# Experts in units of 128 rows instead of tiles of 256, a feed-forward that alternates its two layers by chunk, and a regrouped start and tail

## The chip, the cores and the metric

The kernel runs on one core of one Trainium2 chip. The time is the device time of one execution in microseconds (us); a row of a profile tells times from the first to the last instruction of the profiled execution (its span). The engines are TensorE (PE, with PEld for its weight loads and PEldq for its sequencer, the queue that feeds it), VectorE (DVE), ScalarE (ACT), GpSimd (POOL) and SyncE (SP, which only issues DMAs).

## The reference, cut to what matters

Two blocks are added to x (16 x 256 rows of 256 numbers, with a small vector for each of 16 sequences): a block of a recurrence and a sparse feed-forward, then a block of a mixture and a quantised feed-forward.

```python
# x: (16, 256, 256) f32, cond: (16, 256) f32
# block 1
h_new = tanh(h * (1 - alpha) + sigmoid(h @ Wh.T + z_t @ Wz.T + b) * z_t)     # 256 steps in turn
hs    = all h                                                                # 4096 rows
idx   = top_2(softmax(hs @ gate_w + gate_b))                                 # of 8 experts
h1    = relu(hs @ w1[e] + b1[e])                                             # 256 -> 1024
x     = x + sum over the row's two experts of (h1 @ w2[e] + b2[e])           # 1024 -> 256
# block 2
m     = (shared gated network + two of eight small experts, by sigmoid gates) / 3
q(v)  = clip(round(v / s), 0, 255) * s,  s = max(max(v), 1e-8) / 255         # one s for a whole tensor
h     = relu(q(m) @ wq1.T + bq1)                                             # wq: int8 by row
out   = x + q(h) @ wq2.T + bq2
```

## The kernel before, in words

The program has five stages: the recurrence (to 381 us), the experts (to 814), the mixture (from 829 to 1137), the first pass of the quantised feed-forward (to 1191), which finds the largest hidden value, and its second pass (to 1254), which computes the output. The stages share one program for each engine; each engine runs its instructions in the order in which they stand, and waits for numbered semaphores.

**Experts.** During the recurrence the rows of each expert are scattered into regions of `ROOMS` places in memory. The stage then handles 39 tiles (`SLOT_TILES`) of `ST` = 256 places, so that no tile holds rows of two experts. Which expert a tile has is known only at run time: `value_load` (L1097) brings its number into a register, and the addresses of weights are worked out from it by TensorE's sequencer. `slot_tiles` (L1059) writes out 15 tiles (`JOBS`), loops over 11 x 2 (`Fori`) and writes out the last 2. In each tile:
- TensorE, `experts_pe` (L1079): first layer (L1105), 8 chunks `f` of 128 hidden numbers, each 6 matmuls with `W1` stationary and the tile's 256 rows moving (fp16 high and low parts of weights and rows, without low by low); then 8 transposes of the next tile's rows (L1086); then the second layer (L1117), 8 x 3 x 2 matmuls with `hid` stationary, `SQ` = 2 blocks of 128 rows, and 256 columns of `W2` moving. `hid` and `W1` and their kin are parts of the buffers `lane` and `W`.
- ScalarE: the copy of the transposed rows `xT` (L1129), and for each chunk the relu from `ps` to one of 4 buffers `v4` (L1141). It signals `l1_v`.
- VectorE, `experts_dve` (L1190): for each chunk the high part (L1208) and the low part (L1210) of `hid`, signalling `l1_hid`; the results of the tile before (L1198, signalling `out_ready`, for which the second layer waits); in tiles written out, jobs (`split_piece`, `scale_piece`, `quantise_piece`) that prepare weights of later stages.
- SyncE loads rows (L1406) and biases; GpSimd stores the results by a scatter for each block of 128 rows (L1284) and, in early tiles, scatters rows and pads.

**Feed-forward.** Groups of 512 rows, 8 in all. First pass: ScalarE scales a group (L940) and copies its transposed rows (L935); TensorE transposes (L871) and computes two groups per `row_max` (L875, matmuls L883); VectorE takes maxima (L986). Second pass: `group` (L915) runs all 8 chunks of `hidden` (L906, matmuls L911) of the next group, then waits for the output bank (`ob_s`) and runs all 32 output matmuls (L924) of its own. ScalarE scales and rounds (L955, L952), VectorE casts (L1022) and writes outputs (L1010, L1014). At the end GpSimd adds each group to the result in memory by an accumulating DMA (L1055); `x` was stored there before by SyncE (L1459).

**Start.** SyncE loads all of the recurrence's weights, `h0`, `alpha` and the bias before `z`; TensorE starts when all of VectorE's preparations (`prep`) are done. The first loads of the experts' weights (`stage`, issued behind them on SyncE's queue) are needed by ScalarE (L1506) in the first step.

## Time and profile before

| | us |
|---|---|
| median of 3 runs | 1268.68 (1264.85 to 1269.13) |
| profiled execution, its own time | 1267.8 |
| its span, first to last instruction | 1264.8 |
| experts' stretch (381 to 814) | 433 |
| mean granted clock of TensorE | 0.987 |

The profile is of one execution whose own time lies within 0.1% of the median; 3.0 us of it lie around the span. "busy" is the time in which an engine's instructions ran, also while they overlapped; the chain of waits follows the work that ended last backwards through what released it. A row of the sequencer (PEldq) counts register operations, which aren't in the busy time of any engine. Instructions named ISA in an order of instructions are register operations of an address, FUSED_REGOPS in the trace.

### The profile page before, as it was taken

Reading aid. Unit: us, or ns where it says so; the run is one execution under the profiler, and the core shown is the slowest. Engines: PE = TensorE matmul, PEld = TensorE weight load, DVE = VectorE, ACT = ScalarE, POOL = GpSimd, SP = SyncE. Lnnn points to the kernel's source line nnn. Section 1 sums busy time; section 2 is a strip of 40 time slices with the busy share of each in tenths; the row PEclk is TensorE's granted clock in tenths of the full one; section 3 lists DMA queues with packets and bytes.
Section 4 is the critical chain, followed back from the end, with each engine's and each line's share of the span. In section 5 each row is a group of like instructions: output and inputs, shape, how many; then the busy total and the mean of one; then the engine's idle time right before and its main releaser. Section 6 shows DMA issues by size and latency. Waiting matters only on the chain.

```text
span 1264.8 us, 32645 instructions
## 1 busy us (share of the span) xinstructions
PE 1123.6 (89%) x10732; PEld 864.7 (68%) x10733; DVE 892.9 (71%) x3002; ACT 583.3 (46%) x1782; POOL 250.9 (20%) x289
## 2 busy tenths in 40 slices
PE   6777777787768999999999999889999999987895
PEld 4665666565557999998899999746766666763263
DVE  5677677676775587965555555468898889987875
ACT  3555555555553444444444444362445533434373
POOL 1002112112114675343333333300000000001001
PEclk9999999999999999999999999989999999998998
DMA  6222333233233475343333333243000000000035
GB/s 174 76 72 89 90 97 97 82 93 109 71 91 106 102 166 133 91 70 59 58 53 60 62 62 62 36 132 134 2 1 1 0 1 0 1 1 1 1 51 83
DMA packets 57527, 84.36 MB, mean 67 GB/s; under 512 B 7361, under 2 KB 47170, under 8 KB 57410
## 3 DMA queue, kind: packets, MB, share of 16 engines
q1 hardware_dynamic: 41186, 57.94, 16.1%
q0 software_dynamic: 16224, 24.96, 10.9%
q8 instruction: 62, 1.02, 0.3%
q14 instruction: 55, 0.45, 0.1%
HBM read 51.36 MB, written 35.70 MB: 69 GB/s over the span
## 4 chain that ended last, share of the span: by engine, by line
PE 75%; ACT 9%; DVE 9%; issue 3%; DMA 1%; SPq 1%; POOL 0%; DVEq 0%; ACTq 0%; POOLq 0%
PE ps L570 23%; PE ps L1105 16%; PE ps L1117 16%; PE ps L1660 7%; DVE ps L1589 5%; PE ps L1665 4%; ACT work L1516 4%; ACT ps L1511 3%; DVE imax L986 2%; PE ps L924 2%; PE ps L1630 1%; PE ps L1086 1%; ACT W L955 1%; PE ps L1638 1%; PE ps L911 1%
## 5 line engine op out<-in xcount | busy, mean ns | idle before, releaser
L1141 ACT ACTIVATE lane<-ps,b_now 128x256 f32<-128x256 f32 x312 | 147.4, 474 | 240.1 <-PE ps L1105 216.4
L1105 PE MATMUL ps<-lane,W 128*128 128x256 f16 x1872 | 213.3, 274 | 2.2 <-ACT lane L1129 1.3
L1117 PE MATMUL ps<-W,lane 128*128 x1872 | 210.7, 273 | 0.0
L1105 PEld LDWEIGHTS ps<-lane,W 128*128 x1872 | 184.0, 98 | 25.1 <-issue 2.8
L1117 PEld LDWEIGHTS ps<-W,lane 128*128 128x128 f16 x1872 | 181.5, 98 | 20.4
L1660 PE MATMUL ps<-work 128*128 128x16 f16 x2048 | 99.1, 177 | 89.5 <-ACT work L1516 88.8
L1660 PEld LDWEIGHTS ps<-work 128*128 128x128 f16 x2048 | 76.3, 107 | 141.3 <-ACT work L1516 139.9
L1284 POOL DMA_INDIRECT results<-lane,dest x78 | 123.8, 1588 | 231.3 <-DVE lane L1198 195.8
L570 PE MATMUL ps<-W,work 128*128 128x512 f16 x768 | 168.7, 382 | 0.0
L1210 DVE TENSOR_TENSOR lane<-lane 128x256 f16<-128x256 f32 x312 | 133.4, 427 | 10.8
L570 PEld LDWEIGHTS ps<-W,work 128*128 128x128 f16 x768 | 74.9, 98 | 90.1 <-issue 2.2
L570 PE MATMUL ps<-work,W 128*128 128x256 f16 x1152 | 127.1, 273 | 0.0
L570 PEld LDWEIGHTS ps<-work,W 128*128 128x128 f16 x1152 | 112.4, 98 | 13.1
L1198 DVE SCALAR_TENSOR_TENSOR lane<-ps,b_now 128x512 f32<-128x512 f32 x39 | 26.9, 690 | 127.7 <-PE ps L1117 127.7
L1208 DVE CAST lane<-lane 128x256 f16<-128x256 f32 x312 | 90.5, 290 | 24.4 <-ACT lane L1141 24.3
L1630 PE MATMUL ps<-work 128*128 128x128 f32 x256 | 98.3, 490 | 7.5 <-DVE gw_s L1565 7.5
L1603 DVE TENSOR_TENSOR work<-ps,work 128x32 f16<-128x32 f32 x256 | 48.9, 191 | 78.1 <-ACT ps L1518 77.8
L834 DVE SCALAR_TENSOR_TENSOR W<-ps,comb,W 128x256 f32 (+1 forms) x256 | 101.5, 475 | 1.9 <-PE ps L570 1.9
L1589 DVE TENSOR_TENSOR_SCAN ps<-ps,work 128x64 f32<-128x64 f32 x256 | 76.4, 298 | 34.3 <-ACT ps L1511 11.5
L1254 POOL DMA_INDIRECT rows<-work,slot_of x64 | 62.9, 982 | 156.3 <-DVE ps L1589 152.3
L1576 DVE SCALAR_TENSOR_TENSOR work<-ps,alpha,work 128x16 f32<-128x16 f32 x510 | 93.3, 224 | 0.0
L1511 ACT ACTIVATE ps<-ps 128x32 f32<-128x32 f32 x256 | 46.6, 182 | 97.9 <-PE ps L1665 96.7
(214 smaller groups left out, 1533.7 us busy)
## 6 DMA issues: line engine op xcount, KB each, us to landing
lane<-rows SPq DMA_DIRECT2D x39, 257.0 KB
stage<-in_w1T SPq DMA_DIRECT2D x16, 512.0 KB, 3.7
stage<-in_w2T SPq DMA_DIRECT2D x16, 512.0 KB, 4.0
b_now<-in_b SPq DMA_DIRECT2D x39, 128.0 KB
work<-in_zT SPq DMA_DIRECT2D x32, 128.0 KB, 2.2
results<-in_xn SPq DMA_DIRECT2D x32, 128.0 KB
W<-results SPq DMA_DIRECT2D x8, 512.0 KB, 3.8
out<-W SPq DMA_DIRECT2D x8, 512.0 KB, 4.9
```

Source lines behind the costliest of these rows:

```text
L570: last = pe.matmul(dst, lhs(a, k), rhs(b, k), start=(n == 0 and k == ks[0]), stop=(n == 2 and k == ks[-1]))
L834: dve.scalar_tensor_tensor(y[:, GT * g + q], ps[:, bank_of(U_PAIR + GT * p + q), j * D:(j + 1) * D], comb[:, q, 2 * p + j:2 * p + j + 1], ...
L1105: last = pe.matmul(ps[:, f % 4, 0:ST], of_e(W1[:, bass.ds(e, 1), a, k, f * P:(f + 1) * P]), xT[:, p, b, k], start=(i == 0 and k == 0), sto ...
L1117: last = pe.matmul(ps[:, 4 + q, 0:D], hid[:, a, f, q * P:(q + 1) * P], of_e(W2[:, bass.ds(e, 1), b, f]), start=(i == 0 and f == 0), stop=( ...
L1141: act.activation(v4[:, f % 4], ps[:, f % 4, 0:ST], ACT.Relu, bias=b1_now[:, p, f:f + 1], scale=A_SCALE / W_SCALE).then_inc(l1_v, 1)
L1208: dve.tensor_copy(hid[:, 0, f], v4[:, f % 4]).then_inc(split0, 1)
L1210: dve.tensor_tensor(hid[:, 1, f], v4[:, f % 4], hid[:, 0, f], ALU.subtract).then_inc(l1_hid, 1)
L1284: pool.indirect_dma_start(out=results_d, in_=obuf[:, p, q], in_offset=None, compute_op=ALU.add, out_offset=bass.IndirectOffsetOnAxis(ap=de ...
L1576: dve.scalar_tensor_tensor(zs[:, j % 2, c // BATCH, k, :, 1], h[:, k], alpha[:, k:k + 1], z[:, j, k, c:c + BATCH], ALU.mult, ALU.add).then ...
L1589: dve.tensor_tensor_scan(ps[:, 5, 0:2 * DB], ps[:, 6, 0:2 * DB], zs[:, j % 2, s % STEPS_PER_TILE].rearrange("p c b v -> p (c b v)"), 0.0, ...
L1630: pe.matmul(dst, wz[:, k, cols], z[:, slot, k, :], start=(k == 0), stop=False, skip_group_check=True)
L1660: pe.matmul(ps[:, b + m, c:c + BATCH], w[:, k, m * P:(m + 1) * P], hring[:, prev, 0, k, pc:pc + BATCH], start=False, stop=False, skip_grou ...
```

## The change

- Experts: `ST` 128, so `SLOT_TILES` 71, `JOBS` 29 (31 units written out, 40 in the loop), `EARLY` 32. The second layer's accumulator has two banks by turns, so TensorE waits for the results of the unit before last. ScalarE writes 8 buffers `v8`; VectorE makes high and low parts of two chunks (`PAIR`) at once. Jobs, rows and pads are spread one a unit; each unit has one scatter of results.
- Second pass: for each chunk TensorE runs `hidden(g + 1, f)` and then the 4 outputs of chunk `f` of its own group; the last group runs its two halves one behind the other. The wait for `ob_s` stands ahead of both.
- First pass: `row_max(0)` begins with the first group's half; the transposes of later groups stand between its chunks; ScalarE's order is scale 0, scale 1, copy 0, copy 1, scale 2, and so on.
- Tail: the last two groups (`ADDED` = 6 are still accumulated) are made complete by VectorE (x with bias added ahead, `x_with_bias`, behind group 1's hidden chunks) and stored by SyncE. The mixture's last maximum is taken by halves.
- Start: `z`'s first part and the preparation of `Wz` come ahead of all but the weights' load; TensorE begins with `z`'s products.

```diff
-ST = 256
+ST = 128
 SLOT_TILES = (PAIRS + E * (ST - 1)) // ST
-JOBS = 15
-EARLY = 16
+JOBS = 29
+EARLY = 32
+PAIR = 2
@@ experts_pe, second layer
-                if not is_tile(n, 0):
-                    pe.wait_ge(out_ready, n)
+                if not (is_tile(n, 0) or is_tile(n, 1)):
+                    pe.wait_ge(out_ready, n - 1)
                 for f in range(FC):
-                    pe.wait_ge(l1_hid, FC * n + f + 1)
+                    if f % PAIR == 0:
+                        pe.wait_ge(l1_hid, FC // PAIR * n + f // PAIR + 1)
                     for i, (a, b) in enumerate(((0, 0), (1, 0), (0, 1))):
                         for q in range(SQ):
-                            last = pe.matmul(ps[:, 4 + q, 0:D], hid[:, a, f, q * P:(q + 1) * P],
+                            last = pe.matmul(ps[:, 4 + SQ * p + q, 0:D], hid[:, a, f, q * P:(q + 1) * P],
@@ experts_act
-                    act.activation(v4[:, f % 4], ps[:, f % 4, 0:ST], ACT.Relu, bias=b1_now[:, p, f:f + 1],
+                    act.activation(v8[:, f], ps[:, f % 4, 0:ST], ACT.Relu, bias=b1_now[:, p, f:f + 1],
@@ experts_dve
-                    dve.tensor_copy(hid[:, 0, f], v4[:, f % 4]).then_inc(split0, 1)
-                    dve.tensor_tensor(hid[:, 1, f], v4[:, f % 4], hid[:, 0, f], ALU.subtract).then_inc(l1_hid, 1)
+                    dve.tensor_copy(hid[:, 0, pair], v8[:, pair]).then_inc(split0, 1)
+                    dve.tensor_tensor(hid[:, 1, pair], v8[:, pair], hid[:, 0, pair], ALU.subtract).then_inc(l1_hid, 1)
@@ ffn_pe, first pass
-                pe.wait_ge(yq_T, 2 * n + 2)
+                pe.wait_ge(yq_T, 2 * n + 1)
...
+                        if f == 0 and m == 1:
+                            pe.wait_ge(yq_T, 2 * n + 2)
...
+                    if f in (2, 5) and 2 * n + 2 + f // 5 < GROUPS:
+                        transposes(2 * n + 2 + f // 5)
@@ ffn_pe, second pass
             def group(g, buf):
-                if not is_last(g):
-                    hidden(g + 1)
                 if not is_tile(g, 0) and not is_tile(g, 1):
                     pe.wait_ge(ob_s, 2 * (g - 1))
...
+                else:
                     for f in range(FC):
+                        hidden(g + 1, f)
+                        wait_rounded(pe, g, f)
+                        for q in range(GT):
+                            last = output(buf, f, q)
@@ ffn_dve
+            def x_with_bias(g):
+                xg_ = x1[:, GT * g:GT * g + GT]
+                dve.tensor_tensor(xg_, xg_, bq2.rearrange("p (a d) -> p a d", a=1).broadcast_to([P, GT, D]), ALU.add)\
+                   .then_inc(xb_ready, 1)
@@ SyncE, end
+            for n in range(2 * ADDED, 2 * GROUPS):
+                sp.wait_ge(ob, n + 1)
+                sp.dma_start(out[:, 2 * n:2 * n + 2], y[:, 2 * n:2 * n + 2]).then_inc(last_out, 16)
@@ SyncE, start
             sp.dma_start(wst, WT).then_inc(w_in, 16)
-            sp.dma_start(h0[:], h0T).then_inc(w_in, 16)
-            sp.dma_start(alpha[:], alphaT).then_inc(w_in, 16)
+            sp.dma_start(z[:, 0], zT[:, 0]).then_inc(z_in[0], 16)
@@ TensorE, start
-            pe.wait_ge(prep, 8)
+            pe.wait_ge(prep, 2)
```

The first place is TensorE at the head of a tile, the load of the expert's number and the first layer's first chunk. Before (W and lane are the stationary and the moving operand's buffers, the last numbers the instruction's shape):

```order
L1097 TENSOR_LOAD expert_of
L1097 ISA x2
L1105 ISA [waits l1_v,xT_ready]
L1105 MATMUL ps<-lane,W 128x256
L1105 ISA
L1105 MATMUL ps<-lane,W 128x256 x3
L1105 ISA
L1105 MATMUL ps<-lane,W 128x256
L1105 ISA
L1105 MATMUL ps<-lane,W 128x256
```

After:

```order
L1141 TENSOR_LOAD expert_of
L1141 ISA x2
L1149 ISA [waits l1_v,xT_ready]
L1149 MATMUL ps<-lane,W 128x128
L1149 ISA
L1149 MATMUL ps<-lane,W 128x128 x3
L1149 ISA
L1149 MATMUL ps<-lane,W 128x128
L1149 ISA
L1149 MATMUL ps<-lane,W 128x128
```

The same operations stand there in the same number; each matmul moves half as many columns.

The second place is TensorE between the two layers, the transposes and the second layer's first chunks. Before:

```order
L1086 MATMUL ps<-identh,lane 128x128 [waits xg_in0]
L1086 MATMUL ps<-identh,lane 128x128 x7
L1117 ISA [waits l1_hid,out_ready]
L1117 MATMUL ps<-W,lane 128x256 x4
L1117 ISA
L1117 MATMUL ps<-W,lane 128x256 x2
L1117 ISA [waits l1_hid]
L1117 MATMUL ps<-W,lane 128x256 x4
```

After:

```order
L1130 MATMUL ps<-identh,lane 128x128 [waits xg_in1]
L1130 MATMUL ps<-identh,lane 128x128 x3
L1162 ISA [waits l1_hid,out_ready]
L1162 MATMUL ps<-W,lane 128x256 x2
L1162 ISA
L1162 MATMUL ps<-W,lane 128x256
L1162 ISA
L1162 MATMUL ps<-W,lane 128x256 x2
L1162 ISA
L1162 MATMUL ps<-W,lane 128x256
```

The transposes are 4 for 8, and between two register operations stand half as many matmuls; the wait for `l1_hid` comes once for two chunks.

The third place is TensorE in the second pass, in the first group: the hidden layer of group 1 (L911 before, L926 after) and the output of group 0 (L924, L931). Before:

```order
L911 MATMUL ps<-W,lane 128x512 [waits hb_h]
L911 MATMUL ps<-W,lane 128x512
L911 MATMUL ps<-W,lane 128x512 [waits hb_h]
L911 MATMUL ps<-W,lane 128x512
L924 MATMUL ps<-lane 128x256 [waits hb_qd] x8
L924 MATMUL ps<-lane 128x256 x24
L911 MATMUL ps<-W,lane 128x512 [waits hb_h]
L911 MATMUL ps<-W,lane 128x512
```

After:

```order
L926 MATMUL ps<-W,lane 128x512 [waits hb_h]
L926 MATMUL ps<-W,lane 128x512
L931 MATMUL ps<-lane 128x256 [waits hb_qd]
L931 MATMUL ps<-lane 128x256 x3
L926 MATMUL ps<-W,lane 128x512 [waits hb_h]
L926 MATMUL ps<-W,lane 128x512
L931 MATMUL ps<-lane 128x256 [waits hb_qd]
L931 MATMUL ps<-lane 128x256 x3
```

Eight hidden chunks and then 32 outputs have become one hidden chunk, then 4 outputs, by turns.

## Rows read from the trace of the kernel before

**Rows 1.** Busy time (and instructions) of each engine, the experts' stretch:
```profile
core 0: us, PE busy (x) PEld busy (x) DVE busy (x) ACT busy (x) POOL busy (x), PEclk, DMA share, GB/s
381.00:814.00 433.00, 430.13 (x4071) 385.67 (x4071) 268.20 (x754) 186.55 (x354) 179.41 (x186) 1.00 0.39 81
```
**Rows 2.** Chain of waits, one tile (start us, us, what):
```profile
403.97 0.45 PE ps L1086 x8
404.42 5.24 PE ps L1117 x48
409.65 5.24 PE ps L1105 x48
```
**Rows 3.** Weight loads and sequencer by line: count, ns min/median/max, first and last start
```profile
L1105 PEld LDWEIGHTS ps<-lane,W x1872: 95/98/148, 384.0 to 807.9; 128*128 x188
...
L1105 PEldq FUSED_REGOPS  x1248: 46/46/51, 383.9 to 806.6; - x179
...
L1097 PEldq TENSOR_LOAD <-expert_of x39: 297/301/493, 381.4 to 800.9; - x39
```
**Rows 4.** The same view in short stretches, written-out tiles and loop:
```profile
L1117 PEldq FUSED_REGOPS  x15: 46/46/46, 403.2 to 408.1; - x15
...
L1105 PEldq FUSED_REGOPS  x24: 46/46/46, 409.1 to 412.0; - x24
...
L1105 PEldq FUSED_REGOPS  x32: 46/46/46, 682.1 to 686.5; - x32
...
L1117 PEldq FUSED_REGOPS  x16: 46/46/46, 686.9 to 691.4; - x16
...
L1105 PEldq FUSED_REGOPS  x10: 46/46/51, 692.6 to 694.0; - x10
```
**Rows 5.** Chain of waits in the mixture, matmuls of 128 columns:
```profile
851.73 0.89 PE ps L603 x16
```
**Rows 6.** Groups by shape, 376 to 814: busy us, mean ns, idle before:
```profile
L1210 DVE TENSOR_TENSOR lane<-lane 128x256 f16<-128x256 f32 x312 | 133.4, 427 | 10.8
L1208 DVE CAST lane<-lane 128x256 f16<-128x256 f32 x312 | 90.5, 290 | 24.4 <-ACT lane L1141 24.3
L1198 DVE SCALAR_TENSOR_TENSOR lane<-ps,b_now 128x512 f32<-128x512 f32 x39 | 26.9, 690 | 127.7 <-PE ps L1117 127.7
...
L1141 ACT ACTIVATE lane<-ps,b_now 128x256 f32<-128x256 f32 x312 | 147.4, 474 | 240.1 <-PE ps L1105 216.4 <-DVE lane L1210 10.7 <-issue 9.0
L1129 ACT ACTIVATE lane<-ps 128x1024 f16<-128x1024 f16 x39 | 39.9, 1022 | 0.4 <-PE ps L1086 0.4
```
**Rows 7.** Chain of waits, from the experts to the mixture:
```profile
814.50 1.55 POOL results L1284
...
816.36 3.79 DMA results<-lane,dest
```
**Rows 8.** Chain of waits, first pass of the feed-forward:
```profile
1139.83 3.23 ACT W L940 x3
...
1145.96 3.61 PE ps L883 x8
1149.59 5.95 DVE imax L986 x5
```
**Rows 9.** Chain of waits, second pass:
```profile
1200.14 3.49 PE ps L924 x32
1203.63 1.74 PE ps L911 x8
...
1207.65 3.49 PE ps L924 x32
```
**Rows 10.** End of the chain, and landing times of the output's DMAs:
```profile
1253.69 0.86 POOL out L1055
...
DMA to landing us min/median/max: 2.7/5.3/5.7
```
**Rows 11.** Chain of waits, start:
```profile
8.10 4.31 DMA stage<-in_w1T
```

More of the change, by code:

```diff
@@ L32 @@
 RING = 4
+ADDED = GROUPS - 2
 W_SCALE = 256.0
@@ L894, in ffn_pe @@
             largest(0)
-            for n, groups in enumerate((range(0, 3), range(3, 6), range(6, 8), ())):
-                for g in groups:
-                    transposes(g)
+            for g in range(2):
+                transposes(g)
+            for n in range(GROUPS // 2):
                 row_max(n)
@@ L904, in ffn_pe, with hidden @@
             pe.wait_ge(ia_mx, FC * GROUPS // 2)
-            def hidden(g):
-                for f in range(FC):
-                    if not (is_tile(g, 0) and f < 4):
-                        pe.wait_ge(hb_h, FC * g + f - 3)
-                    for k in range(DC):
-                        last = pe.matmul(ps[:, f % 4], w1qT[:, k, f * P:(f + 1) * P], yqT[:, k, bass.ds(GN * g, GN)],
-                                         start=(k == 0), stop=(k == DC - 1))
-                    last.then_inc(hb_ps, 1)
+            def hidden(g, f):
+                if not (is_tile(g, 0) and f < 4):
+                    pe.wait_ge(hb_h, FC * g + f - 3)
+                for k in range(DC):
+                    last = pe.matmul(ps[:, f % 4], w1qT[:, k, f * P:(f + 1) * P], yqT[:, k, bass.ds(GN * g, GN)],
+                                     start=(k == 0), stop=(k == DC - 1))
+                last.then_inc(hb_ps, 1)
@@ L915, in group, with output @@
+            def output(buf, f, q):
+                return pe.matmul(ps[:, 4 + 2 * buf + q // 2, (q % 2) * D:(q % 2 + 1) * D],
+                                 hq[buf][:, f, q * P:(q + 1) * P], w2qT[:, f], start=(f == 0 and q % 2 == 0),
+                                 stop=(f == FC - 1), skip_group_check=True)
             def group(g, buf):
-                if not is_last(g):
-                    hidden(g + 1)
                 if not is_tile(g, 0) and not is_tile(g, 1):
                     pe.wait_ge(ob_s, 2 * (g - 1))
-                for q in range(GT):
-                    for f in range(FC):
-                        if q == 0:
-                            wait_rounded(pe, g, f)
-                        last = pe.matmul(ps[:, 4 + 2 * buf + q // 2, (q % 2) * D:(q % 2 + 1) * D],
-                                         hq[buf][:, f, q * P:(q + 1) * P], w2qT[:, f], start=(f == 0), stop=(f == FC - 1))
-                    if q % 2:
-                        last.then_inc(ob_ps, 1)
@@ L929, in ffn_pe @@
-            hidden(0)
+                if is_last(g):
+                    for half in range(2):
+                        for f in range(FC):
+                            if half == 0:
+                                wait_rounded(pe, g, f)
+                            for q in (2 * half, 2 * half + 1):
+                                last = output(buf, f, q)
+                        last.then_inc(ob_ps, 1)
+                else:
+                    for f in range(FC):
+                        hidden(g + 1, f)
+                        wait_rounded(pe, g, f)
+                        for q in range(GT):
+                            last = output(buf, f, q)
+                            if f == FC - 1 and q % 2:
+                                last.then_inc(ob_ps, 1)
@@ L930, in ffn_pe @@
+            for f in range(FC):
+                hidden(0, f)
             ffn_groups(pe, group)
@@ new lines, in tile @@
+                    dve.tensor_copy(hid[:, 0, pair], v8[:, pair]).then_inc(split0, 1)
+                    dve.wait_ge(split0, FC // PAIR * n + h + 1)
+                    dve.tensor_tensor(hid[:, 1, pair], v8[:, pair], hid[:, 0, pair], ALU.subtract).then_inc(l1_hid, 1)
+                    if isinstance(n, int) and n < len(LAST_OPS):
+                        ops = LAST_OPS[n]
+                        for k in range(ops.start + 2 * h, min(ops.start + 2 * h + 2, ops.stop)):
+                            if k < ROUTE_OPS:
+                                route_op(dve, BATCHES - 1, k)
+                            else:
+                                late_table_op(dve, k - ROUTE_OPS)
@@ L1679, in step @@
                     ranks(pe, i - 1)
-            pe.wait_ge(prep, 8)
+            pe.wait_ge(prep, 2)
             pe.wait_ge(z_in[0], 16)
+            for part in range(3 * DC):
+                if part == 2:
+                    pe.wait_ge(prep, 5)
+                z_part(0, part)
             pe.wait_ge(idents, 11)
-            for part in range(3 * DC):
-                z_part(0, part)
+            pe.wait_ge(gw_split, 2)
             steps = RING * STEPS_PER_TILE
```

193 lines of the change are left out of this document (106 added, 87 removed).

## The prediction

> **What bounds the kernel now.** I read the table of stretches first. In the experts, 433 us and a third of the span, TensorE is busy 430.1 us; the next, VectorE, 62% [rows 1]. The chain of waits says the same tile for tile: 48 pairs (weight load and matmul) of the first layer 5.24 us, 8 transposes 0.45, 48 pairs of the second layer 5.24, without a gap [rows 2]. A pair with 256 columns moving is 5.24/48 = 0.109 us, a tile 10.93, and 39 tiles 426 us. By this view alone, smaller units look like a gain.
>
> The second view is TensorE's sequencer, the queue that feeds the array. The experts' weights are addressed by a register (which expert), and each change of address costs a register operation: 1248 of them in the first layer, 32 a tile [rows 3], and 16 a tile in the second [rows 4]. Where the queue runs free they come 24 in 2.9 us, 2.9/23 = 0.126 us apart, whether one matmul or three lie between them [rows 4]. In the first layer 32 take 4.0 us and the array 5.24: today the sequencer is ahead. It fills the queue and is held back by it, which costs nothing. Of this the busy shares show nothing; the question of this change is whether it stays so.
>
> **Experts, the large part.** Tiles of 256 rows become 71 units of 128. Rooms fall from 9984 to 9088. Per unit the first layer keeps 48 pairs, now with 128 columns; the second has 24 pairs with 256; 4 transposes. Array price of 128 columns with another weight each time: 16 in 0.89 us, 0.0556 each [rows 5]. A unit is 52 x 0.0556 + 24 x 0.109 = 5.51 us on the array, 71 units 391 us, 35 less than now.
>
> The register operations don't halve. The orders of instructions show the first layer's pattern unchanged (operation, 1 pair, operation, 3 pairs, operation, 1, operation, 1, for each of 8 chunks), and the second's with half the pairs behind the same 16. So the sequencer needs for a unit:
> - first layer 32 x 0.126 = 4.0 us, against 48 x 0.0556 = 2.7 for the array: the sequencer sets it;
> - from there past the transposes to the second layer's first operation 0.4 us (686.5 to 686.9) [rows 4];
> - 15 steps of 0.126, 1.9 us (array 24 x 0.109 = 2.6, but it starts with nothing in hand, behind the sequencer, and the queue hides this over the next boundary, where the sequencer is the later one);
> - from the last operation of the second layer past the load of the expert's number (0.30 us) [rows 3] to the next first layer 1.0 us (408.1 to 409.1) [rows 4].
> Sum 7.3 us for the units that are written out. In the loop the first layer's 32 take 4.4 us (682.1 to 686.5; more register arithmetic stands there), the boundary 1.2 (691.4 to 692.6) [rows 4], and I take 2.3 for the second layer with its own arithmetic: 4.4 + 0.4 + 2.3 + 1.2 = 8.3. 31 units are written out, 40 run in the loop: 31 x 7.3 + 40 x 8.3 = 558 us against 426: **+132 us**. Ends: the operation's pitch alone and a boundary half hidden, 7.0 and 8.0, give 537; waits that each add a little, 7.5 and 8.7, give 581.
>
> The other engines fit in 7.3 us. VectorE per unit: 4 x (0.29 + 0.43) [rows 6], results half of 0.69, so 3.2, and a job of at most some 3 us in some early units. ScalarE: 8 activations of 128 columns and a copy, under half of 8 x 0.47 + 1.02 [rows 6] plus fixed parts, about 4. GpSimd: one scatter of 1.55 [rows 7] where two stood, with loads of numbers; rows and pads, one a unit. The store lands 3.8 us after its issue [rows 7], with two buffers for two units. Waits that vanish (the accumulators' second bank, 8 intermediate buffers for 4) were worth nothing: TensorE never waited for them. The first unit's transposes and copy are half as long: 8 x 0.0556/2 plus half of a copy of 1.02 [rows 2, 6], -0.7, with the issue **-0.9**. The scan carries a table twice as long: 16 columns more in a few operations, **+0.4**.
>
> **Experts to mixture.** The last store is one scatter, not two: 816.36 - 814.50 = 1.86, less some of the issue behind it, with half of the results' 0.69 [rows 6, 7], **-2.1** (0 to -2.2).
>
> **First pass of the feed-forward.** Before, ScalarE scales three groups (3.23 us), then copies and scales in turn, and the first chunk starts at 1145.96 [rows 8]. Now the order is scale, scale, copy, copy: the first half may start near 1139.83 + 2/3 x 3.23 + 1.02 for a copy of 1024 columns [rows 6] = 1143.0, the second a copy later, 1144.0. From 1149.59 on VectorE's maxima set the pace (5 in 5.95 us, 1.19 each, 32 in all) [rows 8] and are what they were. So the start moves by 2 to 3 us and nothing behind it; the other transposes fall between chunks where TensorE waits for VectorE anyway. I take **-2.2**, between 0 and -3.0.
>
> **Second pass.** Now a group takes 7.51 us, from 1200.14 to 1207.65, of which the array works 3.49 in 32 output pairs and 16 x 0.218 = 3.48 in the hidden layer (8 in 1.74) [rows 9], 6.97 together. The rest is a wait for ScalarE at the seam between the two. Alternating by chunk hides it behind the output of the group before: 7 x 0.52 = 3.6 gained. Against it: the wait for the output bank (ob_s) now stands ahead of the hidden layer, and with it all of group 3's hidden chunks are queued; VectorE reaches it later by two additions of 128x1024, each 2 x 0.69 = 1.38 at most by the results' rate for 512 [rows 6]. I charge 1.6 for what of 2.7 isn't covered. The last group by halves puts up to one such addition more behind the last matmul, 0.6. At the start, group 0's output no longer waits for the last two hidden chunks of group 1, 4 x 0.218 = 0.9. Together **-2.3** (0 to -4).
>
> **Tail.** The last accumulating DMA takes 0.86 to issue and lands after 5.3 in the median; a store without accumulation lands after 2.7 at the least [rows 10]. 5.3 + 0.86 - 2.7 - 0.4 of SP's issue, **-3.0** (-1 to -4). **Start:** z's weights first lets TensorE begin earlier, but the first step waits for the load issued at 8.10 that lands 4.31 later [rows 11], and it stands as far behind in SP's queue as before: **0**. The mixture is untouched.
>
> Sum: 1267.8 + 132 - 0.9 + 0.4 - 2.1 - 2.2 - 2.3 - 3.0 = **1389.7**, by the profiled execution (span 1264.8 and 3.0 around it), which lies 0.9 under the median; 1390.
>
> **Rivals.** *A: the sequencer doesn't set the pace*, because its pitch is longer only under the profiler's recording, or the queue lets the array catch up. Then 426 - 391 = -35 and the other edits' -10.1: 1267.8 - 45.1 = **1223**. For it: today's profiled time equals the unrecorded ones, but today the sequencer has slack, so this proves nothing. Against it: 0.126 is found at each free stretch, and 48 operations a unit need 6.0 us at any order, over 5.51. It decides once the pitch falls under 5.51/48 = 0.115 with the boundaries hidden. 0.08.
>
> *B: A, but a pair with 128 columns costs more than 0.0556*, since the weight load (98 ns [rows 3], now hidden under 109) no longer fits. Upper bound 0.098: a middle of 0.077 gives 52 x 0.077 + 2.62 = 6.6 a unit, 469, +43 - 10 = **1301**. Against it: the 16 pairs of [rows 5] change weights each time too. 0.03.
> The Trainium skill, "TensorE: Matmul & The Clock Gate", section "Back-to-back issue gap", gives some 81 ns for a sustained pair of 128 columns; that would be an estimate of 6.8 us a unit and about 1315 in rival B. The trace has 0.0556 for 16 in a row, so it disagrees over short runs, and under 7.3 us a unit the rule would be hidden altogether.
>
> *C: the forecast, with a wait on top.* The second layer's last pair of chunks needs activation, cast and subtraction behind the last matmul, 0.3 + 0.29 + 0.43 and the semaphores between: 1.3 us [rows 6], and the sequencer gets there 0.4 + 1.4 behind it. If VectorE is late by results or jobs, 0.7 a unit is lost, 50 us: **1440**. 0.06.
>
> *D: the pace is as forecast but the loop's units cost what the others do*, 71 x 7.3 = 518: 1350. It lies just under the forecast's range; 0.03.
>
> **How the numbers follow.** The forecast 0.80 (1358 to 1422: the ends 537 and 581 with the small terms' ends), A 0.08, B 0.03, C 0.06, D 0.03. Faster by over 0.5% (about what a measurement of this kernel can tell) is A and a rest of others, 0.09; within 0.5% only something between A and B, 0.02; slower 0.89. The range that holds 8 in 10: 1350 to 1425.
>
> **What would show it.** In the profile after: register operations of the first layer 0.124 to 0.128 apart with the array idle between ("issue" or the sequencer as what ended the wait), a unit of 7.3 us written out and 8.3 in the loop, the experts' stretch 560 us with TensorE busy under 75% of it. The first maximum of the first pass 2 us nearer the mixture's end; groups of the second pass 7.0 us apart but for one; end of the kernel 3 us nearer the last addition. The prediction is wrong if units take 5.5 us with operations closer than 0.115 (A), if the chain names VectorE ahead of the second layer (C), or if the array's pairs are further apart than 56 ns while the sequencer is ahead (B).

## The result and the profile after

The changed kernel takes 1388.44 us (1386.84 to 1389.26) against 1267.72: the ratio is 1.0954, with an interval of 1.093 to 1.0977. It is slower by 121 us, as forecast; 1390 was predicted. The execution that was profiled took 1388.98 us and the three others 1386.84 to 1389.26, so the recording of the profile isn't what makes the kernel slow (one of the two ways in which rival A could have come true).

The spans of the two profiled executions differ by 121.7 us (1386.5 and 1264.8). Cut at the same events in both traces, that is:

| from ... to | before | after | difference | predicted |
|---|---|---|---|---|
| start to the last step of the recurrence | 380.2 | 379.5 | -0.7 | +0.4 |
| to the last matmul of the experts | 433.3 | 565.8 | +132.5 | +131.1 |
| to the mixture's first activation | 10.5 | 8.3 | -2.2 | -2.1 |
| mixture, to its last maximum | 313.7 | 315.0 | +1.4 | 0 |
| first pass | 53.7 | 50.0 | -3.7 | -2.2 |
| second pass, to the last addition | 62.1 | 60.6 | -1.5 | -2.3 |
| to the end of the span | 11.3 | 7.3 | -4.0 | -3.0 |

The busy time of the experts' stretch, which answers to [rows 1] (columns as there):

```profile
381.00:945.30 564.30, 531.28 (x5407) 416.72 (x5403) 274.68 (x727) 243.19 (x641) 172.69 (x236) 0.99 0.31 65
```

The stretch is 131 us longer, and TensorE still counts as busy for 94% of it. I had forecast under 75%, and that was wrong. A "busy" matmul of 128 columns lasts 224 ns in the records while the array takes a new one every 56 ns if it gets one. When they come 90 ns apart the records still overlap, and TensorE looks busy though it waits for its sequencer. The busy share can't tell these apart; the pitch can. The chain of waits, for two written-out units, answers to [rows 2]:

```profile
453.05 4.28 PE ps L1149 x48
457.33 0.22 PE ps L1130 x4
457.55 2.62 PE ps L1162 x24
460.17 0.06 issue
460.23 4.33 PE ps L1149 x48
```

A unit takes 460.23 - 453.05 = 7.18 us. The second layer's pairs cost 2.62/24 = 0.109 as before and the transposes 0.22/4 = 0.055. But the first layer's 48 pairs take 4.28 us, 0.089 each, where the same shape in the mixture took 0.0556 [rows 5]. The rows of the sequencer (count, ns min/median/max, first and last start), over the stage, in a first layer written out and in a first and a second layer of the loop, answer to [rows 3, 4]:

```profile
L1149 PEldq FUSED_REGOPS  x2272: 46/46/51, 382.3 to 942.1; - x190
...
L1162 PEldq FUSED_REGOPS  x1136: 46/46/46, 391.4 to 944.3; - x190
...
L1149 PEldq FUSED_REGOPS  x31: 46/46/46, 452.9 to 456.9; - x31
...
L1149 PEldq FUSED_REGOPS  x32: 46/46/51, 706.4 to 710.9; - x32
...
L1162 PEldq FUSED_REGOPS  x16: 46/46/46, 711.1 to 713.3; - x16
```

3408 operations stand where 1248 + 624 stood; 2272/71 = 32 and 1136/71 = 16 a unit. In the written-out unit 31 of them take 4.0 us (4.0/30 = 0.133 apart; the row's window ends ahead of the 32nd), in the loop 32 take 4.5. By the load of the expert's number, one unit to the next, the written-out units are 7.12 to 7.30 us apart once the first few are past (predicted 7.3), those of the loop 8.24 and 8.42 by turns, 8.33 in the mean (predicted 8.3).

### The profile page after: what moved, and what is told of

Its sections match the earlier page's. It is cut to its first block, busy times and chain, and to the rows that moved or that the text cites. A ratio compares the mean times of both kernels' runs of the same rounds, so it can differ in the third digit from the quotient of the medians.

```text
span 1386.5 us, 38626 instructions
## 1 busy us (share of the span) xinstructions
PE 1222.3 (88%) x12072; PEld 897.1 (65%) x12073; DVE 902.5 (65%) x2980; ACT 645.0 (47%) x2070; POOL 242.2 (17%) x336
## 4 chain that ended last, share of the span: by engine, by line
PE 77%; DVE 8%; ACT 7%; issue 5%; DMA 1%; SPq 0%; another core or an unknown queue 0%; DVEq 0%; ACTq 0%
PE ps L1149 23%; PE ps L576 20%; PE ps L1162 14%; PE ps L1713 7%; DVE ps L1642 4%; PE ps L1718 4%; ACT work L1566 3%; ACT ps L1561 3%; PE ps L926 2%; PE ps L931 2%; DVE imax L1017 2%; PE ps L1683 1%; PE ps L1130 1%; PE ps L897 1%; DVE W L840 1%
## 5 line engine op out<-in xcount | busy, mean ns | idle before, releaser
L1186 ACT ACTIVATE lane<-ps,b_now 128x128 f32<-128x128 f32 x568 | 207.2, 368 | 318.6 <-PE ps L1149 285.6
L1149 PE MATMUL ps<-lane,W 128*128 128x128 f16 x3408 | 325.0, 224 | 33.0 <-issue 27.5
L1149 PEld LDWEIGHTS ps<-lane,W 128*128 x3408 | 241.5, 98 | 125.7 <-issue 54.2
L1256 DVE CAST lane<-lane 128x256 f16<-128x256 f32 x284 | 86.0, 303 | 178.6 <-ACT lane L1186 168.3
L1162 PE MATMUL ps<-W,lane 128*128 x1704 | 198.8, 273 | 0.0
L1162 PEld LDWEIGHTS ps<-W,lane 128*128 128x128 f16 x1704 | 162.6, 98 | 20.9
L1325 POOL DMA_INDIRECT results<-lane,dest x71 | 112.0, 1577 | 170.8 <-DVE lane L1245 165.6
L1258 DVE TENSOR_TENSOR lane<-lane 128x256 f16<-128x256 f32 x284 | 121.1, 427 | 9.7
L1245 DVE SCALAR_TENSOR_TENSOR lane<-ps,b_now 128x256 f32<-128x256 f32 x71 | 30.1, 424 | 99.7 <-PE ps L1162 99.6
```

Source lines behind the costliest of these rows:

```text
L1149: last = pe.matmul(ps[:, f % 4, 0:ST], of_e(W1[:, bass.ds(e, 1), a, k, f * P:(f + 1) * P]), xT[:, p, b, k], start=(i == 0 and k == 0), sto ...
L1162: last = pe.matmul(ps[:, 4 + SQ * p + q, 0:D], hid[:, a, f, q * P:(q + 1) * P], of_e(W2[:, bass.ds(e, 1), b, f]), start=(i == 0 and f == 0 ...
L1186: act.activation(v8[:, f], ps[:, f % 4, 0:ST], ACT.Relu, bias=b1_now[:, p, f:f + 1], scale=A_SCALE / W_SCALE).then_inc(l1_v, 1)
L1258: dve.tensor_tensor(hid[:, 1, pair], v8[:, pair], hid[:, 0, pair], ALU.subtract).then_inc(l1_hid, 1)
L1325: pool.indirect_dma_start(out=results_d, in_=obuf[:, p, q], in_offset=None, compute_op=ALU.add, out_offset=bass.IndirectOffsetOnAxis(ap=de ...
```

## The experiments

Twelve more kernels were run. The three with addresses by constants, the two doses and the one without the loop were timed once each, the other six four to ten times; where a time is of one execution, the trace's stage stands beside it. "Stage" below is the time from the last step of the recurrence to the last matmul of the experts, from the trace; it is 433.3 before and 565.8 in the changed kernel.

### Is it the register operations?

**All of them away, units of 128.**

```diff
-                                             of_e(W1[:, bass.ds(e, 1), a, k, f * P:(f + 1) * P]), xT[:, p, b, k],
+                                             W1[:, 0, a, k, f * P:(f + 1) * P], xT[:, p, b, k],
...
-                                             of_e(W2[:, bass.ds(e, 1), b, f]), start=(i == 0 and f == 0),
+                                             W2[:, 0, b, f], start=(i == 0 and f == 0),
```

> The changed kernel, but TensorE addresses the weights of expert 0 for every unit, by constants; so all rows go through expert 0's weights, and the 48 register operations a unit are gone. The load of the expert's number and the waits stay. Sequencer theory: the array sets the pace, 52 x 0.0556 + 24 x 0.109 = 5.5 us, with the boundary (load of the number, about 1 us of the sequencer) hidden behind what is queued: units of 5.5 to 6.2 us, the stage 565 us - 71 x 1.9 = about 430, the kernel 1240 to 1290. Rival (a pair of 128 columns costs more than 0.0556 in this layer, or waits between the engines hold it): the unit stays above 6.8 us and the kernel above 1330.

Measured: 1226.99 us, against 1265.03 for the kernel before on the same chip; the stage is 406.2 us. The chain in it:

```profile
452.22 2.75 PE ps L1149 x48
454.96 0.22 PE ps L1130 x4
455.19 2.62 PE ps L1162 x24
457.81 2.75 PE ps L1149 x48
```

A unit takes 5.59 us. The first layer's pair costs 2.75/48 = 0.057 in this very layer. So the array's price of a pair was right, and the 4.28 us were not the array's. This is rival A's world (1223 predicted for it), made true by taking away what the forecast rests on.

**The same for tiles of 256**, the edit the same in the kernel before.

> The kernel before (tiles of 256), but TensorE addresses the weights of expert 0 by constants for all tiles, so all rows go through expert 0's weights; no register operations for the weights. Sequencer theory: it was ahead of the array anyway, so nothing is gained: stage 433 us, total within 4 us of before. Rival (register operations cost the array in any case): up to 48 x 0.126 = 6 us a tile less, at least -50 us in all.

Measured: 1263.21 against 1263.65, the stage 432.1 us. Taking 48 register operations from each tile gains nothing where the sequencer is ahead of the array. The two together settle it: the same edit is worth 160 us of the stage in one kernel (565.8 to 406.2) and 1.2 us in the other (433.3 to 432.1).

**Only the second layer's away, units of 128.**

```diff
-                                             of_e(W2[:, bass.ds(e, 1), b, f]), start=(i == 0 and f == 0),
+                                             W2[:, 0, b, f], start=(i == 0 and f == 0),
```

> The changed kernel, but only the second layer's weights are addressed by constants (expert 0), 16 register operations of 48 gone. Sequencer theory: the second layer's operations take 1.9 of the unit's 7.2 us of the sequencer, and what is left for it is to pass 24 pairs on: units of 5.7 to 6.4 us, -60 to -110 us, 1280 to 1330. Rival (the first layer's pairs set the pace by themselves): the second layer doesn't matter as long as the array does its 2.62, units of 7.0 and more, above 1375.

Measured: 1316.87 us, the stage 497.0, a written-out unit mostly 6.4 to 6.5 us, one of the loop 7.3. The chain:

```profile
452.16 2.62 PE ps L1162 x24
454.79 3.58 PE ps L1149 x48
458.37 0.22 PE ps L1130 x4
458.59 2.62 PE ps L1162 x24
```

This is 72 us less than the changed kernel (69 by the stage), at the small end of the expected gain, with units a little longer than the 6.4 that were its end. The place of the gain is instructive: the second layer takes 2.62 us with or without its operations. The first layer became shorter, from 4.28 to 3.6, since the sequencer now runs ahead during the second layer and starts the first with a filled queue. 16 operations of 0.126 are 2.0 us; of these 0.75 came out of a written-out unit and 1.1 out of one of the loop. In the written-out units the trace shows where the rest went, to a wait that the operations had covered: the second layer's last two chunks must have gone through ScalarE and VectorE before the sequencer gets past them. VectorE's last subtraction of the unit, and the sequencer's load of the next unit's number (from two views):

```profile
459.14 0.43 DVE L1258 TENSOR_TENSOR lane<-lane 128x256 f16<-128x256 f32 x1
...
L1141 PEldq TENSOR_LOAD <-expert_of x1: 306/306/306, 459.6 to 459.6; - x1
```

The subtraction signals at 459.576 and the load starts at 459.631, 0.055 us behind, and it does so within 0.001 us in all written-out units from the fourth to the 29th. The signal comes 1.53 us behind the first layer's last register operation. This is the wait of rival C, which becomes the limit of the sequencer once the 16 operations no longer fill the time. In the loop, where the load starts 0.15 and 0.55 us behind the signal by turns, it wasn't taken apart.

### More of them in the kernel before

If the forecast is right, the kernel before has a reserve, and it can be used up. A register that always holds 1 is loaded in each tile, and `hid` is addressed through it, for its low part only (16 operations more) or for both parts (30 more).

```diff
+                z = pe.value_load(one_i[0:1, 0:1], min_val=0, max_val=1)
...
-                            last = pe.matmul(ps[:, 4 + q, 0:D], hid[:, a, f, q * P:(q + 1) * P],
+                            last = pe.matmul(ps[:, 4 + q, 0:D],
+                                             of_e(hid_all[:, bass.ds(z + FC * a + f - 1, 1), q * P:(q + 1) * P])
+                                             if (a or f) and (a == 1) else hid[:, a, f, q * P:(q + 1) * P],
```

> The kernel before (tiles of 256), with 16 or 17 more register operations a tile in the second layer (hid's low part addressed through a register that holds a constant, loaded in each tile); the computation is the same. Sequencer theory: its need rises from 7.3 to 9.9 us a tile written out and from 8.3 to 10.9 in the loop, still not above the array's 10.93: 0 to +12 us. Rival (each register operation costs the array something, slack or not): +17 x 0.126 x 39 = +84 us.

> As the one before, with 30 more register operations a tile (both parts of hid). Sequencer theory: 7.3 + 30 x 0.126 + 0.9 = 12.0 us a tile written out, 13.0 in the loop, against 10.93: 17 x 1.1 + 22 x 2.1 = +64 us (40 to 90). Rival (slack or not, each costs): twice the dose before, +148 us. If register operations don't matter: 0.

Measured: 1274.13 and 1342.35 us, against 1265.03: +9.1 and +77.3 (by the stage +8.8 and +78.7). A first dose of 16 leaves most written-out tiles at 10.9 us (10.87 to 10.98) and lengthens those of the loop from 10.92 to 11.33 in the mean. The second dose gives 12.14 written out (12.0 expected) and 13.0 to 14.3 in the loop (13.0 expected, so my figure for the loop was low). The price per operation isn't constant: 9.1/39/16 = 0.015 us each for the first 16, then (1342.35 - 1274.13)/39/14 = 0.125 us each, a full pitch, for the 14 more. In the chain of the second, the cost stands at the head of each tile, where the queue has run empty:

```profile
437.69 5.24 PE ps L1123 x48
442.93 0.95 issue
443.88 5.44 PE ps L1111 x48
449.32 0.45 PE ps L1088 x8
```

The lines of the page for the first layer in both, where "issue" is what ended the idle time ahead of TensorE (its last column, us):

```profile
L1111 PE MATMUL ps<-lane,W 128*128 128x256 f16 x1872 | 214.0, 275 | 6.4 <-issue 5.0
```
```profile
L1111 PE MATMUL ps<-lane,W 128*128 128x256 f16 x1872 | 227.6, 285 | 52.9 <-issue 51.7
```

5.0 us with the first dose, 51.7 with the second; before, all causes together made 2.2. A tile with 256 columns has so much array work per operation that a late sequencer shows as idle time. With 128 columns it shows as wider pitch instead. (The doses also load the register that holds 1 in each tile, which the forecast of the second dose counted with 0.9 us; this load wasn't tried alone.)

### The loop

`slot_tiles` with all 71 units written out:

```diff
-            for n in range(JOBS):
-                tile(n, n // 2, n % 2)
-            with eng.Fori(0, (SLOT_TILES - 2 - JOBS) // 2) as i:
-                tile(2 * i + JOBS, i + JOBS // 2, 1)
-                tile(2 * i + JOBS + 1, i + JOBS // 2 + 1, 0)
-            for n in range(SLOT_TILES - 2, SLOT_TILES):
+            for n in range(SLOT_TILES):
                 tile(n, n // 2, n % 2)
```

> The changed kernel with all 71 units written out, no loop. Sequencer theory: the loop's extra register arithmetic and branch are the whole difference of 8.33 and 7.22 us a unit, so all units take 7.2: 71 x 7.22 and the first ones: -40 x 1.1 = -44 us, 1340 to 1350. Rival (the loop's units are slower for their data or transfers, or longer code costs as much in fetching): no gain or under 15 us.

Measured: 1344.26 us, the stage 522.3 us, units of 7.09 to 7.33 us throughout after the first ones. The loop's own register arithmetic and branch cost 1.1 us a unit in a kernel whose sequencer is the bound, and the longer code nothing that shows. In the kernel before, the loop's tiles took 10.92 us and the others 10.93: there the loop was free.

### The rest of the change without the units of 128

The kernel before with all the other parts: start, the mixture's last maximum by halves, first pass, second pass, tail.

```diff
-ST = 128
+ST = 256
...
-                    pe.wait_ge(out_ready, n - 1)
+                    pe.wait_ge(out_ready, n)
...
-                    act.activation(v8[:, f], ps[:, f % 4, 0:ST], ACT.Relu, bias=b1_now[:, p, f:f + 1],
+                    act.activation(v4[:, f % 4], ps[:, f % 4, 0:ST], ACT.Relu, bias=b1_now[:, p, f:f + 1],
```

(the diff is from the changed kernel; the rest of the experts' functions, the tables' sizes and the places in `lane` are those of the kernel before too).

> The kernel before, tiles of 256 rows as they were, with all the other parts of the change (start, first pass, maximum by halves, second pass by chunks, the last two groups stored by SyncE). If the experts alone cost +132 and the rest works by itself, the rest is worth what its stages showed, -0.7 (scan), -3.7 (first pass), -1.5 (second pass), -4.0 (tail) and +0.2 (maximum in two parts, on VectorE's path): -9.7, about 1258. The mixture took 1.4 us longer in the changed kernel: if that comes from the units of 128 ahead of it, it is gone here; if it comes from another part of the change, it stays and the sum is -8.5. Rival: the parts lean on the experts' new rhythm or memory places, and less than half of it stays: above 1263.

Measured: ratio 0.9921 (0.9907 to 0.9934), 1257.50 us against 1267.51: -10.0 us. So the rest is a gain, and it doesn't hang on the units of 128. Its stages against before, by the trace: first pass -4.0, second pass -1.5, end -5.8, mixture +1.0, experts +1.1. The mixture's surplus stayed, and the sum is still -10, since the end brought more than the 4.0 that were expected of it.

The mixture's surplus is thus not from the units of 128, and it isn't from the other parts either: it lies between +0.1 and +1.7 us in every kernel run here, also in those that change nothing but the first pass, the second, the tail, the start or the doses. Most of it in the changed kernel's profiled execution is the clock of TensorE. In the wait between the stages the granted clock fell to the lower level (1.2 GHz); it was back at the higher (2.4 GHz) 8.6 us behind the mixture's first activation before, and 10.6 us behind it after. The stretches of 2 us around this, one of before and two of after (columns as in [rows 1]; the third number from the end is the granted clock as a share of 2.4 GHz):

```profile
831.98:833.98 2.00, 2.00 (x9) 0.83 (x8) 0.96 (x2) 0.60 (x1) 0.00 (x0) 0.86 0.02 3
```
```profile
961.57:963.57 2.00, 2.00 (x6) 0.71 (x5) 0.69 (x1) 0.60 (x1) 0.00 (x0) 0.50 0.03 10
963.57:965.57 2.00, 2.00 (x10) 0.82 (x9) 1.26 (x5) 0.05 (x1) 0.00 (x0) 0.85 0.39 101
```

In the first of these, 8 to 10 us behind the first activation, TensorE began 9 matmuls at 0.86 and 6 at 0.50, having been busy throughout the 2 us ahead in both. ScalarE's activations lie at the same distance from the first one in both traces until 8.0 us; the next, at 11.0 before, comes 1.0 later after, and those behind it stay 0.9 to 1.2 later. So 1.0 of the 1.4 us is the clock's. What the rest is stays open: with the second dose the clock was back at 8.5 us and the mixture still took 0.8 longer.

**First pass alone:**

```diff
-                pe.wait_ge(yq_T, 2 * n + 2)
+                pe.wait_ge(yq_T, 2 * n + 1)
...
+                    if f in (2, 5) and 2 * n + 2 + f // 5 < GROUPS:
+                        transposes(2 * n + 2 + f // 5)
```

> The kernel before, with the first pass alone changed (half a pair first, transposes between chunks, ScalarE's order). If the 3.7 us that its stage lost in the changed kernel are its own: -3 to -4 us. If part of it came with the maximum by halves or the experts: -1.5 to -2.5, as predicted from the start alone.

Measured: ratio 0.9972 (0.9962 to 0.9981), 1264.76 us, -2.8; by the trace the stage is 3.75 us shorter, as expected and within what the interval allows (2.4 to 4.8 us).

**Second pass alone:**

```diff
+                    for f in range(FC):
+                        hidden(g + 1, f)
+                        wait_rounded(pe, g, f)
+                        for q in range(GT):
+                            last = output(buf, f, q)
```

> The kernel before, with TensorE's second pass by chunks alone (the wait for the output bank at the head of the group, last group by halves). By the changed kernel's trace a group fell from 7.51 to 7.16 us, and the stall of 1 us in the second group is put down to the two additions of x with bias, which aren't here: -2.0 to -3.2 us. If that stall comes from the wait's new place instead, -0.5 to -1.5.

Measured: ratio 0.9982 (0.9973 to 0.9992), 1265.15 us, -2.4; by the trace the stage is 2.14 us shorter.

**Tail alone:**

```diff
+            def x_with_bias(g):
+                xg_ = x1[:, GT * g:GT * g + GT]
+                dve.tensor_tensor(xg_, xg_, bq2.rearrange("p (a d) -> p a d", a=1).broadcast_to([P, GT, D]), ALU.add)\
+                   .then_inc(xb_ready, 1)
...
+            for n in range(2 * ADDED, 2 * GROUPS):
+                sp.wait_ge(ob, n + 1)
+                sp.dma_start(out[:, 2 * n:2 * n + 2], y[:, 2 * n:2 * n + 2]).then_inc(last_out, 16)
```

> The kernel before, with the end alone changed (x with bias by two additions, the last two groups stored by SyncE). The changed kernel's time from the last addition to the end was 4.0 us shorter (11.3 to 7.3), and the additions cost up to 2.4 us on VectorE in the second pass: -2 to -4 us. If the shorter end came from the second pass's new order, -1 or less.

Measured: ratio 0.9961 (0.9946 to 0.9976), about -5 us; by the trace the end is 5.7 us shorter and the second pass unchanged (62.2 against 62.1). The two additions cost nothing here; more was gained than the changed kernel's 4.0 and than the 2 to 4 that were expected, which the part on the tail below explains.

**Start alone:**

```diff
             sp.dma_start(wst, WT).then_inc(w_in, 16)
-            sp.dma_start(h0[:], h0T).then_inc(w_in, 16)
-            sp.dma_start(alpha[:], alphaT).then_inc(w_in, 16)
+            sp.dma_start(z[:, 0], zT[:, 0]).then_inc(z_in[0], 16)
```

> The kernel before, with the start alone changed (z's first part and the preparation of Wz first, TensorE begins with z's products). By the chain the first step waits for the load of an expert's weights that lands at 12.4 us in both: 0, within -0.4 and +0.4 us. If the recurrence's 0.7 us less in the changed kernel comes from here, -0.7.

Measured: ratio 1.0006 (0.9996 to 1.0015): nothing. In the changed kernel the chain of the start has the same transfer at its end as [rows 11], issued at the same time:

```profile
8.10 4.16 DMA stage<-in_w1T
12.28 0.32 ACT W L1556
```

So the 0.7 us in the table above aren't the start's. With no edit to the recurrence, its last step starts at 377.0 us in one profiled execution (the second dose) and at 380.9 in another (the first pass alone). Most of this goes with the chip: on two of them it lies at 377.0 to 378.3 in all eight kernels run there, on a third at 379.4 to 380.9 in four.

### The seam in the second pass

In the form with all parts, one seam between groups is longer than the others, where group 2's outputs and the hidden chunks of group 3 begin:

```profile
1206.23 0.45 PE ps L926 x2
...
1206.78 0.79 ACT W L986
1207.56 0.20 issue
1207.77 0.60 PE ps L926 x2
```

From the start of the two matmuls at 1206.23 to that of the next at 1207.77 it is 1.54 us, where 0.87 is usual and 1.07 at the other seams of the loop. The edit sets the additions apart:

```diff
-                    if is_tile(g, 0):
+                    if is_tile(g, 0) or is_tile(g, 1):
                         dve.wait_ge(bq_ready, 3)
-                        for k in range(ADDED, GROUPS):
-                            x_with_bias(k)
+                        x_with_bias(ADDED + g)
```

> Tiles of 256 with all the other parts of the change, and the two additions of x with bias no longer one behind the other in the first group but one each behind the hidden chunks of groups 1 and 2. If the 1.0 us by which the second group's first hidden chunks come late is the 2.4 us block of additions on VectorE, each of 1.2 now fits into VectorE's slack of a group: -0.5 to -1.1 us against the undivided form (1257.5), 1256.4 to 1257. If it comes from the wait for the output bank whatever VectorE does, the same as the undivided form or, with two small stalls, up to 1 us more.

Measured: ratio 0.992 (0.9907 to 0.9934), 1251.77 us against 1263.65 for the kernel before beside it; the undivided form had 0.9921, the same within the intervals. The trace has the gain, though: the second pass takes 59.99 us for 60.62, and the seam is now like any other:

```profile
1200.73 0.44 PE ps L931 x4
1201.17 0.05 issue
1201.22 0.60 PE ps L926 x2
```

The long seam was the block of additions, and 0.6 us is what it cost in the end. By time alone the two forms can't be told apart; they are the fastest of the kernels that compute the whole reference, 0.8% under the kernel before.

## Why the prediction was right

**The bound and its change: right, by its own numbers.** 71 units of 7.3 and 8.3 us were forecast; 7.2 and 8.33 came. The step that carried it was to count register operations in the two orders of instructions and to price them at a place where the sequencer ran free [rows 4]. The array's price from [rows 5] held as well (0.057 where 0.0556 was said, seen only once the operations were away). The terms held one by one: written out (means of the 7th to 28th unit) the first layer's operations take 4.1 us, the way to the second layer 0.2, its operations 2.0, the way to the next unit 0.9, for 4.0, 0.4, 1.9 and 1.0 in the forecast; in the loop 4.5, 0.2 to 0.4, 2.2 and 1.1 to 1.5, for 4.4, 0.4, 2.3 and 1.2. One bound was added up wrongly: with 537 us and the small terms at their lower ends the forecast's range begins at 1365, not at 1358. It changes nothing in the outcome.

**The rivals.** A (the array sets the pace) and B (a pair of 128 columns costs more) fall together: in the first run the array did its pairs in 0.057, and 81 ns, which the Trainium skill's "TensorE: Matmul & The Clock Gate", section "Back-to-back issue gap", gives for a sustained stream, wasn't met by 48 in a row at 57 ns. C (a wait for VectorE on top) didn't come, the second layer ran in 2.62 us without a gap, but it was near: VectorE's last signal comes 1.53 us behind the first layer's last operation (1.3 was forecast), and in the unit above the sequencer reached the operation that needs it at 1.73, 0.2 us later. D was wrong as to the loop and right as to its size: written out it is 1344, for 1350.

**The transition:** -2.2 for -2.1, one store's instruction less.

**First pass: right sign, the size off by 1.5.** The prediction said the start moves by 2 to 3 us "and nothing behind it". The row of the maxima (first and last start), before and after:

```profile
L986 DVE TENSOR_REDUCE imax<-ps x32: 1211/1223/1225, 1147.9 to 1187.5; 128x1 f32<-128x1024 f32 x32
```
```profile
L1017 DVE TENSOR_REDUCE imax<-ps x32: 1214/1224/1226, 1277.0 to 1314.7; 128x1 f32<-128x1024 f32 x32
```

Counted from the mixture's end (1137.60 and 1268.56), the first came at 10.3 and comes at 8.4: -1.9, as said. But from the first to the last it was 39.6 us and is 37.7, 1.22 a maximum (five in a row came 1.19 apart [rows 8]). Before, VectorE had waited once for 1.9 us and once for 0.5 in between, while TensorE did the transposes of the next groups in one piece, with a wait for GpSimd's copy of a group among them. From the chain of before:

```profile
1156.62 0.46 PE ps L871 x8
...
1157.21 1.05 POOL W L1051
...
1158.30 0.62 PE ps L871 x8
```

I had taken VectorE's pace from those five and hadn't counted all 32. The first pass alone has the same 37.7 us.

**Second pass: -1.5 for -2.3.** The seams were the step that failed. I let 0.52 us a group vanish; a group of the loop takes 7.16 us now (1351.14 - 1343.98 in the chain), so 0.35 vanished and 0.19 stayed:

```profile
1343.98 0.60 PE ps L926 x2
...
1351.14 0.60 PE ps L926 x2
```

The two matmuls at the seam take 0.60 instead of 0.43, at each of the loop's four seams. The trace shows what ends last there: the wait for the output bank, which now stands ahead of the hidden layer. VectorE's scaling of that bank, and the sequencer's operation that waits for it (from two views):

```profile
1343.04 0.68 DVE L1043 TENSOR_TENSOR W<-ps,W 128x512 f32 x1
...
L924 PEldq FUSED_REGOPS  x1: 46/46/46, 1343.8 to 1343.8; - x1
```

The bank is free at 1343.73, 0.06 us behind the start of the last output matmul. The sequencer runs this operation and one more, and the next matmul starts at 1343.98, 0.31 behind the last one instead of 0.11. The wait alone would have cost nothing, as the seam ahead of group 6 suggests, which is written out and has no register operation behind the wait: there the bank is free at 1365.13, the last output matmul started at 1365.15 and the next one starts at 1365.26. So it is again the sequencer, kept from running ahead by a wait; that the operations behind it are the reason rests on this one comparison. Four seams of 0.2 are 0.8 us. Two more terms were mis-sized: the stall by the additions was charged with 1.6 and was worth 0.6, and the trace of before has six seams to gain from, not seven.

**Tail: -4.0 for -3.0, by another mechanism.** I took the landing of SyncE's store for the end. The rows of the block's end (line L100 in the changed kernel; start and length of GpSimd's DRAIN) say otherwise:

```profile
L100 POOLq DRAIN  x1: 6607/6607/6607, 1379.6 to 1379.6; - x1
...
L100 SPq DRAIN  x1: 7/7/7, 1382.2 to 1382.2; - x1
```

SyncE is done at 1382.2. GpSimd, whose last accumulating DMA has landed by 1379.5, then drains for 6.6 us and ends the kernel. Before, that DMA was group 7's and the drain took 5.0:

```profile
L98 POOLq DRAIN  x1: 4974/4974/4974, 1259.6 to 1259.6; - x1
```

The gain was that the last accumulating DMA is of an earlier group. In the tiles of 256 the drain takes 4.8 us with the same tail, which is why the end is 5.7 us shorter there: the changed kernel gave 1.8 of them back to a longer drain. By an estimate from these rows (groups 7.2 us apart), with one more group stored by SyncE the drain would start near 1372.4 and end before SyncE's store, for one addition more of 1.2 us on VectorE. That wasn't tried.

**Mixture and recurrence:** +1.4 and -0.7 where 0 and +0.4 stood. 1.0 of the +1.4 is the clock's later return in the profiled execution; the -0.7 is less than the recurrence differs between chips, so the +0.4 for the longer table is neither shown nor refuted by any run. The two nearly cancel. That the sum came out within 2 us is partly luck: measured less predicted, the seven stages are -1.1, +1.4, -0.1, +1.4, -1.5, +0.8 and -1.0, which cancel to -0.1.

## What to carry to other kernels

Halving a tile halves the array's work for each instruction, but not the register operations that address it; where addresses are known only at run time, count these per tile in the order of instructions and set (count x pitch) against the array's time before cutting a tile. A sequencer that is ahead is a reserve that no busy share shows, and what goes beyond it costs in full: 16 operations more a tile cost 9 us, 30 cost 77. A wait that ends late at the head of a group keeps the sequencer from running ahead, and the register operations behind it can then show (0.2 us a seam in the second pass). Take the pace of a stage from the first and the last of all its instructions, not from a few in a row, and look at which engine's drain ends the kernel.

## What the runs showed of the hardware that was not expected

- TensorE counts as busy for 94% of a stretch in which it could do its work in 0.72 of the time (a stage of 406.2 us for 565.8), as the records of matmuls (224 ns) overlap at any pitch below that.
- A register operation of TensorE's sequencer is 46 ns long in the records and comes at least 0.124 us after the one before in the changed kernel (0.123 in the kernel before, 0.119 with the second dose), with one matmul or three between; the 48 of a unit, the number's load and the boundaries make 7.2 us.
- GpSimd's drain at the end is constant to the nanosecond for a program and differs between them: 4974 ns in the kernel before and its variants with 8 accumulated groups, 4811 with 6, 6607 in all the kernels with units of 128. What it depends on is open.
- The recurrence runs as fast at the lower clock level as at the higher. Before and after, the whole stretch (columns as in [rows 1]):

```profile
12.70:381.00 368.30, 278.09 (x3762) 219.60 (x3761) 258.86 (x1410) 199.38 (x1114) 50.00 (x59) 1.00 0.31 92
```
```profile
12.70:381.00 368.30, 278.70 (x3771) 219.78 (x3772) 259.91 (x1411) 198.88 (x1112) 50.72 (x59) 0.50 0.30 88
```

  The granted clock is 1.00 in one and 0.50 in the other, and 256 steps take 367.3 and 366.7 us. The level fell in the start of the changed kernel (0.97 in the first 12.7 us) and stayed low until the experts. Of the kernels with an unchanged start, four ran it at 0.50 too (the first dose, the second pass alone, the tail alone, tiles of 256 by constants), so the change isn't its cause. The three other executions of the changed kernel had a mean clock of 0.988 to 0.990 and took 1386.84 to 1389.26 us, where the profiled one with 0.853 took 1388.98: a mean clock of 0.853 instead of 0.987 for the whole kernel says nothing about where 121 us went.
